# Decoder layer on Trainium2: the tiles' up products as three fp32r products, weights divided beside the alignment, twelve row buffers

## The reference

```python
x = x + attn(layernorm(x))                    # gated recurrence along the 64 positions; itself adds its input
x = x + align(ctx_1024, layernorm(x))         # per sequence: 64x64 distances, time warping, path, gather
x = x + ffn(layernorm(x))                     # shared expert and one of 7 routed experts per token

def ffn(x):
    swiglu = lambda h, w1, w2, w3: silu(h @ w1.T) * (h @ w3.T) @ w2.T      # 128 -> 352 -> 128
    probs = sigmoid(clip(x @ router_w.T + routing_bias, -50, 50))
    p, sel = top_1(probs)                      # weight and expert of each token
    switched = sum over e of where(sel == e, p, 0) * swiglu(x, ew1[e], ew2[e], ew3[e])
    total = clip(0.5 + p + 1e-8, 0.5, 2)
    return 0.5 / total * swiglu(x, sw1, sw2, sw3) + switched / total
```

## Time and profile before

| | us |
|---|---|
| median of 3 runs | 319.24 (317.83 to 319.77) |
| the profiled execution | 317.4, its span 316.2 |
| stage 1 | 0 to about 82 |
| stage 2 | to about 129 |
| stage 3 | to about 222 |
| stage 4, 38 tiles | to 316.2 |
| PE busy over the span | 233.6 |
| DVE busy | 198.9 |
| POOL busy | 154.9 |
| ACT busy | 135.6 |

### The profile page before, as it was taken

One profiled execution on the slowest core, in us unless ns is written; L12 is line 12 of the kernel. 1 busy time (PEld: TensorE's weight loads), 2 busy tenths in 40 slices (PEclk: granted clock), 3 DMA queues, 4 the chain that ended last, 5 costly groups with the idle time before them and its releaser, 6 DMA issues.

```text
span 316.2 us, 5406 instructions
## 1 busy us (share of the span) xinstructions
PE 233.6 (74%) x1335; PEld 169.9 (54%) x1337; DVE 198.9 (63%) x819; ACT 135.6 (43%) x374; POOL 154.9 (49%) x229
## 2 busy tenths in 40 slices
PE   0076598987200004969999999998899999999993
PEld 0033366776200001437757666667677787878782
DVE  0479999883079998877787756573544454544441
ACT  1467558655261120478654432220344444343441
POOL 7166777566300000033147777270066676767676
PEclk9999979999955555999999999999999999999998
DMA  7999402121400000000012122072333434434440
GB/s 206 315 333 394 156 3 43 41 60 43 114 4 0 0 2 1 0 1 3 0 42 68 45 84 87 17 177 75 78 39 51 59 55 54 66 48 64 52 42 3
DMA packets 35662, 23.12 MB, mean 73 GB/s; under 512 B 8385, under 2 KB 32961, under 8 KB 35521
## 3 DMA queue, kind: packets, MB, share of 16 engines
q1 hardware_dynamic: 27720, 18.15, 20.6%
q0 software_dynamic: 6496, 4.24, 9.5%
q10 hardware_dynamic: 1416, 0.40, 0.6%
HBM read 14.53 MB, written 8.50 MB: 73 GB/s over the span
## 4 chain that ended last, share of the span: by engine, by line
PE 40%; POOL 19%; DVE 18%; issue 11%; DMA 5%; ACT 4%; ACTq 2%; SPq 0%; POOLq 0%; DVEq 0%
POOL out L1089 18%; PE bank L810 6%; PE bank L812 6%; PE bank L798 6%; PE bank L309 3%; PE bank L311 2%; PE bank L330 2%; PE bank L578 2%; PE bank L677 2%; PE bank L717 2%; PE bank L373 2%; DMA bo<-in_b_o 2%; DVE R L546 2%; DVE junk L583 2%; DVE bn L161 2%
## 5 line engine op out<-in xcount | busy, mean ns | idle before, releaser
L1089 POOL DMA_INDIRECT out<-loan,xs x38 | 58.8, 1548 | 42.2 <-DVE loan L1082 39.0
L170 POOL TENSOR_TENSOR rstds<-ve,half 128x4 f32<-128x4 f32 x24 | 27.7, 1156 | 42.4 <-DVE ve L168 37.6
L1073 DVE TENSOR_TENSOR loan<-bank,loan 128x352 f32<-128x352 f32 x38 | 19.9, 524 | 36.5 <-PE bank L1016 36.5
L789 POOL DMA_INDIRECT routed<-pay,pos_i x32 | 31.6, 987 | 16.2 <-ACT loan L814 5.9
L1057 ACT COPY h_ffn<-bank 128x256 f32<-128x256 f32 x38 | 14.2, 373 | 46.3 <-PE bank L1041 46.3
L1031 PE MATMUL bank<-w_sb,h_ffn 128*128 (+1 forms) x228 | 31.8, 275 | 1.4 <-ACT h_ffn L1058 1.4
L1031 PEld LDWEIGHTS bank<-w_sb,h_ffn 128*128 128x128 f32 (+1 forms) x228 | 28.6, 191 | 7.5 <-issue 7.0
L814 ACT ACTIVATE loan<-bank 128x512 f32<-128x512 f32 (+1 forms) x24 | 14.3, 594 | 38.3 <-PE bank L810 29.6
L1015 PE MATMUL bank<-w_sb,xsT 128*128 x76 | 28.9, 462 | 0.0
L1016 PE MATMUL bank<-w_sb,xsT 128*128 x76 | 28.7, 459 | 0.0
L798 PEld LDWEIGHTS bank<-w_sb,h_ffn 128*128 128x128 f32 (+1 forms) x192 | 22.6, 191 | 5.1 <-DVE h_ffn L822 1.9
(11 more groups left out here) (209 smaller groups left out, 546.9 us busy)
## 6 DMA issues: line engine op xcount, KB each, us to landing
w_sb<-in_w SPq DMA_DIRECT2D x8, 352.0 KB, 7.6
xs<-routed SPq DMA_DIRECT2D x38, 65.0 KB, 2.1
xr<-in_x SPq DMA_DIRECT2D x8, 256.0 KB, 5.8
cn<-in_ctx SPq DMA_DIRECT2D x8, 256.0 KB, 6.2
cT<-in_ctxT SPq DMA_DIRECT2D x8, 256.0 KB, 6.1
out<-xr SPq DMA_DIRECT2D x8, 256.0 KB, 2.5
w_sb<-in_w SPq DMA_DIRECT2D x8, 192.0 KB, 9.3
dist<-d SPq DMA_DIRECT2D x7, 128.0 KB, 2.0
```

Of the source, the lines that this page charges most:

```text
L170: return pool_done(pool.tensor_tensor(rstds[:, k, s], ve[:, k, s], half[:, s], ALU.pow))
L789: pool.indirect_dma_start(routed, bass.IndirectOffsetOnAxis(ap=pos_i[:, n:n + 1], axis=0), pay[:, n, :], None, bounds_check=TABLE - 1).the ...
L1073: dve.tensor_tensor(g[:, i, 0:HID], U[i][:, 0:HID], g[:, i, 0:HID], ALU.mult).then_inc(s_h, 1)
L1089: pool.indirect_dma_start(out_rows, bass.IndirectOffsetOnAxis(ap=xs[:, s % XB, ROW - 1:ROW].bitcast(U32), axis=0), y[:, s % 4, :], None, b ...
```

## The change

The shared expert's up weights move to a tensor of their own, `w13_sh`, and stay fp32. The seven routed experts' up weights are divided in stage 2 into a high part in fp32r (a cast on ACT) and a low part: PE makes identity x weights minus identity x high part in a PSUM bank, ACT casts that to fp32r. This is done in ten blocks of 512 columns (the last of 320), at rows 4 to 7 and 16 to 21 of the warping, a block's low part one row after its high part. 20 keep-busy products stand ahead of them. In stage 4 each up product becomes three fp32r products that add up in the same bank (`three`: high x high, high x low, low x high), and the rows of a tile are divided too: ACT casts the high part from PSUM, DVE subtracts it for the low part. To make room, the raw weights and the warping's tables lie at the other end of SBUF and are given up before stage 3. `XB`, the number of row buffers, goes from 8 to 12; the last store of x3 stays behind the eighth load. In stage 3 the `align` of the next chunk moves from the head of a turn to behind the logits of the turn before, `step` in odd turns moves ahead of the mask, and the norm of chunk 0 goes from ACT (with two POOL steps ahead) to DVE.

Left out of the diff: `sb` passes on the argument `side`; `d2` moves to the other end too; `w13_sb[:, SH, ...]` becomes `w13_sh` in the load and in `up`; the semaphores' names; `keep_busy` was defined further down; PE no longer waits for the loads of the up weights ahead of stage 4.

```diff
         xr = sb("xr", [P, NT, D])
-        w13_sb = sb("w13_sb", [P, NE + 1, 2 * HID])
+        early = ExitStack()
+        w13_sb = sb("w13_sb", [P, NE, 2 * HID], at=early, side="right")
+        w13_sh = sb("w13_sh", [P, 2 * HID])
+        minus_r = sb("minus_r", [P, P], F32R)
         w2_sb = sb("w2_sb", [P, NE + 1, KC, D])
...
         RR = 4
-        near = sb("near", [P, HT2, T])
-        dd = sb("dd", [P, HT2, T])
+        near = sb("near", [P, HT2, T], at=early, side="right")
+        dd = sb("dd", [P, HT2, T], at=early, side="right")
         R = sb("R", [P, RR, T + 1])
...
         loan = sb("loan", [P, NT, D])
+        w13_hi = sb("w13_hi", [P, NE, 2 * HID], F32R)
+        w13_lo = sb("w13_lo", [P, NE, 2 * HID], F32R)
...
+            act_done(act.mul(minus_r[:, :], ident[:, :], -1.0))
             fetch_table(ACT.Sqrt)
...
+            def keep_busy(count):
+                for _ in range(count):
+                    pe_done(pe.matmul(bank[5][:, :], warm[:, 0:P], warm[:, :], start=True, stop=True))
             m_nl, m_up, m_gate, m_stop, m_dF = ({} for _ in range(5))
+            hi_flat, lo_flat = (w[:, :, :].rearrange("p e h -> p (e h)") for w in (w13_hi, w13_lo))
+            raw_flat = w13_sb[:, :, :].rearrange("p e h -> p (e h)")
+            LOW = bank[2:5] + bank[6:8]
+            splits = -(-NE * 2 * HID // CW)
+            weights = {}
+            def block(k):
+                return slice(k * CW, min((k + 1) * CW, NE * 2 * HID))
+            def high_part(k):
+                a = block(k)
+                after(act, m_w13[a.start // (2 * HID)], m_w13[(a.stop - 1) // (2 * HID)])
+                weights["hi", k] = act_done(act.copy(hi_flat[:, a], raw_flat[:, a]))
+                o = LOW[k % len(LOW)][:, 0:a.stop - a.start]
+                after(pe, m_w13[a.start // (2 * HID)], m_w13[(a.stop - 1) // (2 * HID)], weights.get(("lo", k - len(LOW))))
+                pe_done(pe.matmul(o, ident[:, :], raw_flat[:, a], start=True, stop=False))
+                pe.wait_ge(*weights["hi", k])
+                weights["rest", k] = pe_done(pe.matmul(o, minus_r[:, :], hi_flat[:, a], start=False, stop=True))
+            def low_part(k):
+                a = block(k)
+                act.wait_ge(*weights["rest", k])
+                weights["lo", k] = act_done(act.copy(lo_flat[:, a], LOW[k % len(LOW)][:, 0:a.stop - a.start]))
...
                     gates(gates_at[i])
+                if i == 0:
+                    after(pe, m_warm)
+                    keep_busy(20)
+                if 4 <= i < 8 or 16 <= i < 16 + splits - 4:
+                    k = i - 4 if i < 16 else i - 12
+                    high_part(k)
+                    if k:
+                        low_part(k - 1)
+                if i == 16 + splits - 4:
+                    low_part(splits - 1)
                 if i in stops_at:
...
         mk = sb("mk", [P, 2, CT, P])
+        early.close()
         xT = sb("xT", [P, TOK])
...
         shift = sb("shift", [P, NT])
-        XB = 8
+        XB = 12
         xs = sb("xs", [P, XB, ROW])
         h = sb("h_ffn", [P, 2, KC, CW])
-        xsT = sb("xsT", [P, 2, P])
+        xs_hi = sb("xs_hi", [P, 2, P], F32R)
+        xs_lo = sb("xs_lo", [P, 2, P], F32R)
         s_put, s_x3 = sem("s_put"), sem("x3_out")
...
             m = mark("x2", c, dve_done(dve.tensor_tensor(xr[:, s, :], ALIGN[:, :].rearrange("p (t d) -> p t d", d=D), xr[:, s, :], ALU.add)))
-            m = ln_stats(2, c, m)
+            m = mark("rstd", c, ln_stats(2, c, m))
+            if c == 0:
+                return
             after(pool, m)
...
+            if c == 0:
+                dve.wait_ge(*old("rstd", c))
+                for t in range(CT):
+                    m = normalise(2, t, pay[:, t, 0:D])
+                mark("norm", c, m)
+                return
             act.wait_ge(*old("shift", c))
...
             mark("xT", c, act_done(act.copy(xT[:, c * CW:(c + 1) * CW], X_T[:, :])))
+        def three(o, left, right):
+            (a_hi, a_lo), (b_hi, b_lo) = left, right
+            pe.matmul(o, a_hi, b_hi, start=True, stop=False, skip_group_check=True)
+            pe.matmul(o, a_hi, b_lo, start=False, stop=False, skip_group_check=True)
+            return pe.matmul(o, a_lo, b_hi, start=False, stop=True, skip_group_check=True)
...
         distance_to_middle(0)
         distance_to_middle(1)
         mask(0)
+        align(0)
         for turn in range(NC + 2):
             odd_turn = turn % 2 == 1
             here = (turn - 3) // 2 if odd_turn else (turn - 4) // 2
+            if odd_turn:
+                step(here - 1)
             if turn + 1 < NC:
                 mask(turn + 1)
+            if turn == 1:
+                normed(0)
             if turn < NC:
-                align(turn)
                 add_aligned(turn)
-            if odd_turn:
-                step(here - 1)
-            else:
+            if not odd_turn:
                 step(here)
             put_rows(4)
-            if 1 <= turn <= NC:
+            if 2 <= turn <= NC:
                 normed(turn - 1)
             if turn >= 2:
                 next(expert)
-            else:
-                keep_busy(3)
             if turn + 2 < NC:
                 distance_to_middle(turn + 2)
+            if turn == 0:
+                keep_busy(4)
+            if turn == 1:
+                keep_busy(9)
             if 1 <= turn <= NC:
                 turned(turn - 1)
                 keep_turned(turn - 1)
             if turn >= 2:
                 logits(turn - 2)
-            if odd_turn:
-                if here >= 0:
-                    routing[here] = route(here)
-                step(here)
-            else:
-                step(here)
+            if odd_turn and here >= 0:
+                routing[here] = route(here)
+            step(here)
+            if turn + 1 < NC:
+                align(turn + 1)
             if turn >= 3:
                 next(expert)
-            elif turn < 2:
-                keep_busy(3)
             step(here)
         last = NG - 1
         while not old("pos", last):
...
                     sp.load(row_reg, rows_at[0:1, s:s + 4])
-                if s == XB:
+                if s == XB - 4:
                     store_x3(NC - 1)
...
                         pe.wait_ge(s_h, s - 1)
-                    pe.matmul(A[i][:, 0:HID], xsT[:, i, :], w13_flat[:, bass.ds(base, HID)], start=True, stop=True).then_inc(s_a, 1)
-                    pe.matmul(U[i][:, 0:HID], xsT[:, i, :], w13_flat[:, bass.ds(base + HID, HID)], start=True, stop=True).then_inc(s_u, 1)
+                    left = xs_hi[:, i, :], xs_lo[:, i, :]
+                    three(A[i][:, 0:HID], left, (hi_flat[:, bass.ds(base, HID)], lo_flat[:, bass.ds(base, HID)])).then_inc(s_a, 1)
+                    three(U[i][:, 0:HID], left, (hi_flat[:, bass.ds(base + HID, HID)], lo_flat[:, bass.ds(base + HID, HID)])).then_inc(s_u, 1)
                 if k == 0:
...
+            def high_x(s):
+                act.wait_ge(s_x, s + 1)
+                act.copy(xs_hi[:, s % 2, :], X[s % 2]).then_inc(s_xh, 1)
+            for s in range(2):
+                high_x(s)
             for s in range(NS + 1):
...
                     act.activation(g[:, i, 0:HID], A[i][:, 0:HID], ACT.Silu).then_inc(s_g, 1)
+                if s + 2 < NS:
+                    act.wait_ge(s_u, s + 1)
+                    if s >= 2:
+                        act.wait_ge(s_y, s - 1)
+                    high_x(s + 2)
                 if s >= 1:
...
-            def copy_x(s):
-                dve.wait_ge(s_x, s + 1)
-                dve.tensor_copy(xsT[:, s % 2, :], X[s % 2]).then_inc(s_xT, 1)
+            def low_x(s):
+                dve.wait_ge(s_xh, s + 1)
+                dve.tensor_tensor(xs_lo[:, s % 2, :], X[s % 2], xs_hi[:, s % 2, :].bitcast(F32), ALU.subtract).then_inc(s_xT, 1)
             for s in range(2):
-                copy_x(s)
+                low_x(s)
             for s in range(NS + 2):
...
                 if s + 2 < NS:
-                    copy_x(s + 2)
+                    low_x(s + 2)
                 if s >= 2:
```

More of the change, by code:

```diff
@@ L220, in program @@
             m_rt = load(sp, rt[:, :], router, "rt_in")
-            m_w13 = {e: load(sp, w13_sb[:, e, :], w13[:, e, :], f"w13_in{e}") for e in range(NE, -1, -1)}
+            m_w13 = {e: load(sp, w13_sb[:, e, :] if e < NE else w13_sh[:, :], w13[:, e, :], f"w13_in{e}") for e in range(NE, -1, -1)}
             m_w2 = {e: load(sp, w2_sb[:, e, :, :], w2[:, e, :, :], f"w2_in{e}") for e in range(NE, -1, -1)}
@@ L573, in program @@
             m = dve_done(dve.tensor_scalar(W[:, HT2:HT2 + 1], best[:, :], mirror[:, 0:1], mirror[:, 1:2], ALU.mult, ALU.add))
-            def keep_busy(count):
-                for _ in range(count):
-                    pe_done(pe.matmul(bank[5][:, :], warm[:, 0:P], warm[:, :], start=True, stop=True))
             after(dve, m_dF[len(ROWS) - 1])
@@ L1091, in pool_tiles @@
```

(1 more changed line is left out.)

18 lines of the change are left out of this document (8 added, 10 removed).

## The result

The changed kernel takes **310.54 us** (median of 4 runs, 306.99 to 311.36) against 319.5 us (317.83 to 320.43) for the kernel before in the same series: a ratio of 0.970, 95% interval 0.962 to 0.979. It is faster, by 9.0 us. A second series of the same kernel gave 309.3 us (6 runs, ratio 0.968, 0.964 to 0.973). The profiled execution took 310.51 us, its span is 309.2. That is 6.9 us under the profiled execution before (317.4), where the medians are 9.0 apart: the one profile before is of an execution 2.1 us under its median, the one after lies at its median.

A forecast was written before the change was run, and what follows sets the result against it. PE was taken to set the tile stage's pace, 2.30 us a tile. Terms -9.6 (up products), +0.3 (entry), 0 and -0.3 (turns) sum to -9.6, from median 319.24 to 309.6 us; 8-in-10 range 305 to 317.

The forecast's parts named there:

- Up products: Stage 4 on PE: six fp32r products at 0.155 us replace four fp32 instructions, 0.26 us less a tile, -9.6 us.
- Rivals C: L1015 and L1016: fp32r streams slower than one column per cycle, 0.22 us a product, +4.8 us, 324; chance 0.06.
- E: Up products: fp32r products are issued as pairs like fp32 ones, +87 us; chance 0.01.
- Weight loads: Tile stage on PE: loads go from four to six per tile and lie beside products, no cost.
- rival D: Tile stage: weight loads don't hide, each of six products pays 0.11 us more, +15 us, 334; chance 0.03.
- ACT's cast: Tile stage: the cast is done 0.07 us before the hidden block's copy could start, cost 0.
- Rival A: Tile stage: the cast delays the copies by 0.26 us, loop 2.22 us, only 3 us saved, 316.2; chance 0.09.
- The entry's +0.3: First tile: the chain row, cast, subtraction, product is longer by one step, +0.3 us.
- Twelve buffers: Tile stage's row loads: twelve in flight instead of eight keep a wait from appearing, 0 us.
- Dividing the weights: Alignment stage: ACT's casts leave its gates in time for DVE, cost 0, ends 0 and +2.7 us.
- Rival B: Alignment stage: ACT's casts delay the second gate by up to 2.7 us, 312.3; chance 0.07.
- Turns: Stage 3 routing: chunk 0's norm moved to DVE costs +0.7, moved alignment wins 1.0, together -0.3 us.

The follow-up runs named there:

- four-product kernel: Changed kernel with a fourth fp32r product (low x low) in each up product: 321.47 us, ratio 1.007.
- the cast made twice: Changed kernel with a second ACT cast of the rows' high part, into a tile nobody reads: 308.65 us, ratio 0.966.
- the filled gap: Changed kernel with eight keep-busy products in the 2.0 us in which PE waits for the second chunk's norm: 307.62 us, ratio 0.964.
- work in the gap: Changed kernel with the shared expert's second pair of up products moved ahead of the second turning: 306.36 us, ratio 0.960; repeated 306.32 us.
- the same again: Unaltered repeats: first in the table the changed kernel, 309.3 us, ratio 0.968; later the kernel with up products moved ahead of the second turning, 306.32 us, ratio 0.961.
- without the 20: Changed kernel without the 20 keep-busy products ahead of the weights' division: 308.57 us, ratio 0.968.
- turns as before: Changed kernel with stage 3's turns in the old order, alignment at the head, first norm on ACT: 310.5 us, ratio 0.974.
- 11 keep-busy: Kernel with up products moved ahead of the second turning, 11 instead of 16 keep-busy products ahead of the path's product: 305.60 us, ratio 0.959.
- one product: Changed kernel with only the high parts' product in each up product, casts and subtractions kept: 305.21 us, ratio 0.955.
- the four of the tile kernels: Changed kernel with one stage 4 edit each: one product 305.21 us, four products 321.47, ACT's cast twice 308.65, eight row buffers 315.06.

## Why the prediction was right, and where its terms were off

Forecast 309.6 us, range 305 to 317; measured 310.54, and 309.3 in the second series. The forecast's own mechanism came: PE gets faster, nothing else takes its place. But the number is closer than the working. The forecast put the profiled execution at 307.8 us, 1.8 under the median as before; it took 310.51. Between the two traces the change is -7.0 us, where the terms add up to -9.6. The medians moved by 9.0, and by 9.9 in the second series, so some 2 us of that lie in a difference that the two traces don't hold, and that the forecast hit the median within 1 us is in part luck. Where the longer executions of the kernel before lose those 2 us stays open: only its execution of 317.4 us was profiled. Their mean granted clock is the lower one: in the last series of 11 runs, the five shortest have 0.921 to 0.930 and the four longest 0.916 to 0.920.

By its steps, from the traces:

1. *Up products,* -9.6: **-8.1** (37 x 0.22). The term was mis-sized, its mechanism right. A product steps by 0.160 us where 0.155 was taken; six make 0.96 instead of 0.93, and the tile came to 2.07 instead of 2.04. Both estimates by a bf16 row (0.148) and by a switch paid once were too kind; L327 by ends (0.165) was the closer row. By the Trainium skill, page "TensorE: Matmul & The Clock Gate", section "Back-to-back issue gap", whose formula is given for a single product, it would be 149 ns; the trace has 160, 7% more. What the difference is stays open. The four-product kernel confirms 0.160 from the other side. Rivals C (0.22) and E fall with the same rows.
2. *Weight loads.* Hidden, rival D false: each of 0.19 us lies beside a product, with all rows in use. The Trainium skill, page "TensorE: Matmul & The Clock Gate", section "The mechanism", has loads overlap running products only when the row groups differ; this trace doesn't agree. The same section names the background weight buffer as another case, so that rival D was weaker by the page itself than the forecast has it.
3. *ACT's cast.* The slack of 0.07 us was in truth 0.02 (cast over at 251.90, copy at 251.92). It did not matter: the cast made twice changed nothing. Rival A had its premise nearly met and its price wrong, because it counted a whole ACT instruction, 0.26 us, where a further one takes 0.16, and because the loop has 0.1 us to spare under PE's pace. The entry's +0.3 came: from the first turning of rows to the first up product 1.14 us, 0.83 before.
4. *Twelve buffers,* 0, as a cover. PE never waits for rows, as written, but what the cover is worth was not stated: with eight it is +5.8 us. Eight were just enough for the old pace, with rows that landed as little as 0.4 us ahead.
5. *Dividing the weights,* 0: right. The gates start at 99.03 and 109.66, the long scans at 101.53 and 112.11, each as far from the first scan as before, within 0.1. Rival B did not come: the clock was full again from 97.39 us, ahead of the long row of casts, and two casts pass ACT in 1.0 us, less than 2 x 0.58, as their records overlap. The margin is thinner than this profile shows. In six of the twelve profiles with this division, those where the clock rose 9.9 us or more behind the first scan, the first gate ends only 0.45 to 0.53 us ahead of the long scan that reads it (1.44 in this profile, 0.47 in the changed kernel's second). That is the slack of 0.5 us that was worked out for this case, and no more:

```profile
97.86 0.62 ACT L529 CAST w_hi<-w_sb 128x512 fp32r<-128x512 f32 x1
98.55 0.59 ACT L540 CAST w_lo<-bank 128x512 fp32r<-128x512 f32 x1
99.03 1.06 ACT L546 ACTIVATE gate<-nl 128x1024 bf16<-128x1024 bf16 x1
99.99 0.61 ACT L529 CAST w_hi<-w_sb 128x512 fp32r<-128x512 f32 x1
100.50 0.59 ACT L540 CAST w_lo<-bank 128x512 fp32r<-128x512 f32 x1
100.98 0.63 ACT L529 CAST w_hi<-w_sb 128x512 fp32r<-128x512 f32 x1
...
109.66 0.84 ACT L546 ACTIVATE gate<-nl 128x768 bf16<-128x768 bf16 x1 [3.01 <-DVE nl L579]
```

6. *Turns,* -0.3: **+0.25** (-1.07 and +1.32). The first turning came 1.1 us sooner and the second had 2.0 us of idle ahead of it, both as written. What was missing is the second consequence: that this idle stretch is followed by 3.4 us at half clock, 1.7 us dearer, as the filled gap shows. With that gone, the filled gap's kernel has 92.5 us from path to tiles where the kernel before has 93.9: -1.4, near the bound of -1.7, so that the order by itself is worth more than the -0.3.
7. *The end of stage 2* was not in the sum at all: +0.5. The 16 keep-busy products amid the way back were in no term. In the profile before the clock rose at 126.8, while they ran, and they were over in time; in this one it rose at 128.1, and they stood ahead of the path's product. What sets the moment of the rise stays open; two traces of one program (work in the gap) have it at 125.8 and 128.9, and with them 0.79 and 1.58 us from the way back to the product.

On POOL the idle time before an addition fell from 0.75 to 0.53 us, as written; POOL's floor of 1.85 us was not reached by any kernel here.

## What to carry to other kernels

Find the floor of the loop behind the engine that you speed up before you speed it up: here 1.96 us of loop under 2.30 us of PE, read from the tail, told in advance that at most 0.34 us a tile could be won, however cheap the products. When a loop gets faster, count again how far ahead its loads are issued; the same edit with the old eight buffers would have given less than half. And price an idle stretch of TensorE twice, once for itself and once for a fall of the clock that may follow; real work moved into it took back 3.2 us of the 3.7 here. Last, compare more than one trace of each kernel before a term of half a microsecond is believed.

## What the runs showed of the hardware

**A stretch of idle and the clock.** Starts of the half-clock stretches (granted clock 1.2 GHz instead of 2.4) in stages 2 and 3 and their lengths, us, from the records of each profile, beside PE's idle time ahead of the first and the second turning, each with the 0.16 us noted as a drain:

| kernel | weights' division | before and in the way back | idle ahead of turnings 1, 2 | turns |
|---|---|---|---|---|
| changed | 90.56, 6.8 | 111.05, 17.1 | 0.7, 2.0 | 145.18, 3.4 |
| the same again | 88.93, 10.2 | 109.41, 17.1 | 0.7, 2.0 | 143.54, 3.4 |
| without the 20 | 86.07, 13.7 | 109.96, 17.1 | 0.7, 2.0 | 144.09, 3.4 |
| turns as before | 89.38, 10.2 | 109.86, 17.1 | 3.1, 0 | none |
| gap filled | 91.52, 6.8 | 108.59, 17.1 | 0.7, 0.3 | none |
| work in the gap | 91.70, 6.8 | 112.18, 13.7 | 0.7, 0.3 | none |
| the same again | 91.36, 6.8 | 111.84, 17.1 | 0.7, 0.3 | none |
| 11 keep-busy | 88.48, 10.2 | 108.97, 17.1 | 0.7, 0.3 | none |

In all seven profiles with the 2.0 us gap (the three above and the four of the tile kernels) the clock fell behind it, for 3.4 us in six and for 6.8 with one product, and in none of the four with the gap filled. The gap's length alone does not decide: the kernel with the old turns stood for 3.1 us at a stretch and kept its clock, and so did the kernel before, with 3.3. PE's work behind the two gaps differs, four turnings and then eight small logits products in the changed kernel, four turnings, three keep-busy products and the alignment's eight in the old order; whether that decides was not tested. The moment of the rise differs by 3.1 us between two traces of one program, so that a keep-busy row that fits in one run is too long in the next.

**fp32r.** A product of 352 columns steps by 0.160 us at full clock, 0.013 over one column per cycle (352 / 2.4 = 147 ns), with its weight loads beside it; an fp32 product of the same size took 0.30 per instruction and two instructions. Three fp32r products cost 0.48 us against 0.60.

**ACT.** Two instructions of 128x128 out of PSUM (the copy and the cast of the doubled cast) start 0.16 us apart when they wait for nothing, though each is noted with 0.27.
